# Fewer tile numbers per register load in the source stage, and ranks kept in PSUM in the target stage, of a graph network kernel

## What is computed

```python
h = jnp.maximum(_layernorm(x, axis=-1), 0.0)
x = x + _L0_gnn_ref(h, edge_index, W, att_src, att_dst, bias)   # attention over the edges of a target
h = jnp.maximum(_layernorm(x, axis=-1), 0.0)
# second layer, row = source node, col = target node
msg = jnp.concatenate([x[row], x[col], edge_attr], axis=-1)
h = jax.nn.relu(msg @ W1 + b1)
msg_out = h @ W2 + b2
out = jax.ops.segment_sum(msg_out, row, num_segments=x.shape[0])
```

## Time and profile before

| | us |
|---|---|
| median of three runs | 5765.21 |
| lowest, highest | 5764.62, 5769.41 |
| the profiled execution | 5768.6 |
| its span, first to last instruction | 5766.7 |

### The profile page before, as it was taken

How to read it: one execution, slowest core, us unless ns; L and a number is a source line. 1 busy time by engine, 2 the same in 40 slices (tenths; PEclk the granted TensorE clock), 3 DMA queues, 4 the chain that set the end, 5 groups by cost and what they waited for, 6 DMA issues and landing times.

```text
span 5766.7 us, 160506 instructions
## 1 busy us (share of the span) xinstructions
PE 5126.9 (89%) x34498; PEld 4050.5 (70%) x34499; DVE 3987.0 (69%) x14407; ACT 2886.9 (50%) x8241; POOL 3919.7 (68%) x3713
## 2 busy tenths in 40 slices
PE   4888888888888886999999999999997999999999
PEld 3677777777777774676676666666665777777777
DVE  6788878878877877555455455455445888888887
ACT  3555555555555553333333333332224777777776
POOL 4777777777777775677777777777776555555553
PEclk6888888888888887999999999999998999999999
DMA  4522222222222234998989989989896999999997
GB/s 109 161 53 53 53 53 53 52 53 52 53 52 53 53 96 140 274 274 260 268 257 259 260 261 256 264 247 268 253 256 183 211 214 212 215 214 212 214 214 188
DMA packets 859988, 990.83 MB, mean 172 GB/s; under 512 B 307992, under 2 KB 663224, under 8 KB 859774
## 3 DMA queue, kind: packets, MB, share of 16 engines
q1 hardware_dynamic: 662494, 608.23, 40.6%
q0 software_dynamic: 190592, 378.22, 24.5%
q10 hardware_dynamic: 6816, 3.38, 0.2%
HBM read 726.65 MB, written 262.76 MB: 172 GB/s over the span
## 4 chain that ended last, share of the span: by engine, by line
PE 60%; issue 10%; POOL 10%; DMA 9%; DVE 7%; DVEq 2%; ACT 2%; POOLq 0%; ACTq 0%; SPq 0%
PE bank L1700 13%; PE bank L1532 11%; PE bank L1623 9%; PE bank L1625 8%; PE bank L1690 7%; DMA xr<-arena 6%; POOL arena L495 5%; POOL xr L543 5%; PE bank L1458 2%; DMA arena<-h_tab,arena 2%; PE bank L1613 2%; PE bank L1681 1%; DVE arena L936 1%; DVE arena L1043 1%; DVEq L247 1%
## 5 line engine op out<-in xcount | busy, mean ns | idle before, releaser
L495 POOL DMA_INDIRECT arena<-h_tab,arena x1612 | 1595.4, 990 | 545.1 <-issue 406.8
L543 POOL DMA_INDIRECT xr<-arena x1612 | 1580.7, 981 | 510.6 <-issue 366.4
L1532 PE MATMUL bank<-arena 128*128 128x136 f32 x6448 | 1321.8, 334 | 76.4 <-DVE arena L1043 8.2
L704 ACT ACTIVATE arena<-bank 128x256 f32<-128x256 f32 x1612 | 591.8, 385 | 1403.1 <-PE bank L1625 923.9
L557 POOL DMA_INDIRECT arena<-p_tab,arena x428 | 668.5, 1562 | 658.7 <-DMA arena<-p_tab,arena 457.7
L1623 PE MATMUL bank<-arena 128*128 128x256 f32 x3224 | 1028.6, 401 | 92.4 <-DVE arena L1237 50.5
L1532 PEld LDWEIGHTS bank<-arena 128*128 128x128 f32 x6448 | 990.3, 216 | 159.5 <-issue 65.8
L622 ACT ACTIVATE arena<-bank 128x256 bf16<-128x256 bf16 x1612 | 618.5, 384 | 916.2 <-PE bank L1458 836.9
L1625 PE MATMUL bank<-arena 128*128 128x256 f32 x3224 | 976.4, 385 | 0.0
L1700 PE MATMUL bank<-arena 128*128 128x257 f32 x3424 | 899.0, 385 | 3.0 <-ACT arena L781 2.4
L1043 DVE TENSOR_TENSOR arena<-arena,bank 128x272 f32 x1612 | 692.1, 429 | 168.0 <-PE bank L1532 150.9
(11 more groups left out here) (254 smaller groups left out, 6438.3 us busy)
## 6 DMA issues: line engine op xcount, KB each, us to landing
arena<-xr SPq DMA_DIRECT2D x428, 516.0 KB, 3.9
arena<-q_tab SPq DMA_DIRECT2D x1612, 128.0 KB
arena<-in_edge_attr SPq DMA_DIRECT2D x61, 832.0 KB, 8.9
arena<-rel_tab SPq DMA_DIRECT2D x124, 224.0 KB
arena<-h_tab,arena POOLq DMA_INDIRECT x1612
xr<-arena POOLq DMA_INDIRECT x1612
arena<-rel_tab SPq DMA_DIRECT2D x124, 192.0 KB
xr<-arena SPq DMA_DIRECT2D x26, 516.0 KB
```

What stands on the lines that cost most here:

```text
L495: pool.indirect_dma_start(G[:, q, t, :], None, h_tab, bass.IndirectOffsetOnAxis(ap=idx[:, q, t:t + 1], axis=0)).then_inc(sem(f"gath{q}"), 16)
L543: pool.indirect_dma_start(xr, bass.IndirectOffsetOnAxis(ap=pos[:, q, t:t + 1], axis=0), Rb[:, t, :], None).then_inc(sem(f"scat{m}"), 16)
L1532: last = pe.matmul(PSB[3 + t % 2][:, k * H * MW:(k + 1) * H * MW], OH[:, (t + 2 * q) % 4, k * P:(k + 1) * P], flat(msg[:, t, :, :]), start ...
```

## The change

`pair_bins` takes the first pair and a count now. In a turn VectorE loads eight numbers from pair 8i - 4 on, which starts where it did, and TensorE eight from pair 8i - 1 on, so its loads start three numbers further on; the loads behind the loop take four numbers on VectorE and one on TensorE. In the target stage the sum of line 1203 is written into bank 5 in place; the product reads the sum there, writes `t49`, and only then TensorE gets the bank back: `rk_used` moves from the sum to the product, and a new semaphore `run_added` orders the two.

```diff
--- before.py
+++ after.py
@@ -248,10 +248,10 @@
                 bin_row[0:1, bass.ds(b * RB, count)], engines=[engine], min_val=0, max_val=NT - 1,
                 skip_runtime_bounds_check_because="a node's tile, clamped at 0")[1]
 
-        def pair_bins(engine, i):
+        def pair_bins(engine, first, count=SB):
 
             return nc.values_load_multi_w_load_instructions(
-                pbrow[0:1, bass.ds(i * SB, SB + 4)], engines=[engine], min_val=0, max_val=NT - 1,
+                pbrow[0:1, bass.ds(first + 4, count)], engines=[engine], min_val=0, max_val=NT - 1,
                 skip_runtime_bounds_check_because="counted over the bins, held under their number")[1]
 
 
@@ -1200,20 +1200,21 @@
             def rank(r, m):
                 lo, hi = m * RK, min((m + 1) * RK, BT)
                 dve.wait_ge(sem("rk_ps"), 3 * r + m + 1)
-                V.tensor_tensor(t49[:, lo:hi, :], PSB[5][:, 0:(hi - lo) * NT].rearrange("p (t b) -> p t b", b=NT),
-                                run0.unsqueeze(1).to_broadcast([P, hi - lo, NT]), ALU.add).then_inc(sem("rk_used"), 1)
+                v = PSB[5][:, 0:(hi - lo) * NT].rearrange("p (t b) -> p t b", b=NT)
+                V.tensor_tensor(v, v, run0.unsqueeze(1).to_broadcast([P, hi - lo, NT]), ALU.add).then_inc(sem("run_added"), 1)
 
             def own(r, s, m):
                 lo, hi = m * RK, min((m + 1) * RK, BT)
-                dve.wait_ge(sem("rk_used"), 3 * r + m + 1)
-                V.tensor_tensor(t49[:, lo:hi, :], t49[:, lo:hi, :], oh49[:, s, lo:hi, :], ALU.mult).then_inc(sem("own_ready"), 1)
+                dve.wait_ge(sem("run_added"), 3 * r + m + 1)
+                V.tensor_tensor(t49[:, lo:hi, :], PSB[5][:, 0:(hi - lo) * NT].rearrange("p (t b) -> p t b", b=NT),
+                                oh49[:, s, lo:hi, :], ALU.mult).then_inc(sem("rk_used"), 1)
 
             def total(r):
                 dve.wait_ge(sem("total_ps"), r + 1)
                 V.tensor_tensor(run0, run0, PSB[7][:, 64:64 + NT], ALU.add).then_inc(sem("run_ready"), 1)
 
             def reduced(r):
-                dve.wait_ge(sem("own_ready"), 3 * r + 3)
+                dve.wait_ge(sem("rk_used"), 3 * r + 3)
                 V.tensor_reduce(posf, t49, AX.X, ALU.add).then_inc(sem("posf_ready"), 1)
 
             def places(r, s):
@@ -1358,7 +1359,7 @@
                 V.tensor_tensor(a, a, PSB[4 + m % 2][:, 0:XW], ALU.add).then_inc(sem("accB_done"), 1)
 
             def sources(i, first=False, last=False):
-                regs = pair_bins(ENG.DVE, i)
+                regs = pair_bins(ENG.DVE, SB * i - 4)
                 for m in range(SB):
                     if m < SB - 1:
                         hotp(i, m + 1, first)
@@ -1374,7 +1375,7 @@
             with dve.Fori(1, NTURN - 1) as i:
                 sources(i)
             sources(NTURN - 1, last=True)
-            regs = pair_bins(ENG.DVE, NTURN)
+            regs = pair_bins(ENG.DVE, NPAIR - 4, 4)
             for m in range(SB - 4, SB):
                 if m < SB - 2:
                     add_r(NPAIR - SB + m + 2, m + 2, False)
@@ -1701,11 +1702,11 @@
                 last.then_inc(sem("seg_ps"), 1)
 
             def sources(i, first=False):
-                regs = pair_bins(ENG.PE, i)
+                regs = pair_bins(ENG.PE, SB * i - 1)
                 for m in range(SB):
                     turnp(SB * i + m, m)
                     if not (first and m < 1):
-                        source_rows(SB * i + m - 1, (m - 1) % SB, regs[m + 3], first)
+                        source_rows(SB * i + m - 1, (m - 1) % SB, regs[m], first)
                     if not (first and m < 3):
                         segment(SB * i + m - 3, (m - 3) % SB, first)
             pe.wait_ge(sem("pb_in"), 16)
@@ -1713,8 +1714,8 @@
             sources(0, True)
             with pe.Fori(1, NTURN) as i:
                 sources(i)
-            regs = pair_bins(ENG.PE, NTURN)
-            source_rows(NPAIR - 1, SB - 1, regs[3], False)
+            regs = pair_bins(ENG.PE, NPAIR - 1, 1)
+            source_rows(NPAIR - 1, SB - 1, regs[0], False)
             for m in range(SB - 3, SB):
                 segment(NPAIR - SB + m, m, False)
             pe.wait_ge(sem("accB_done"), NPAIR + 1)
```

## The result

The changed kernel takes 5866.82 us in the median of four runs (5863.24 to 5874.09), the kernel before 5767.31 beside it: a ratio of 1.0172, with 1.0156 to 1.0187 as its interval. It is **1.7% slower, by 99.5 us**, where 5726 and faster was predicted. The profiled execution of after has a span of 5866.1 us against 5766.7.

The account below looks back on a forecast made before the run. The prediction took scatter issue to bound the target stage and TensorE, delayed by register loads at turn ends, the source stage. Its terms -11.2 + 0.7 - 29 = -39.5 gave a median of 5726 us, range 5712 to 5750.

Parts of the forecast that it names:

- Eight registers for twelve: Source stage: four numbers fewer per register load save 320 ns a turn, 33.6 us over 105 loads, -29 us net.
- Rival (4): Source stage: TensorE's load from 8i + 3 costs another half load, 0.42 us a turn; 5799 us, chance 0.04.
- Product from PSUM: Target stage: with one product operand in PSUM the 46 held scatters go, -11.2 us (bounds 0 and -16.6).
- Bank 5 is released later: Next group's matmuls wait for the product, not the sum: 0 in the target stage, +0.7 us in the node stage.
- 4.5 were taken off: Source stage: part of the register loads' gain comes back as longer waits for rows, 4.5 us.
- the prediction's own sign: Source stage: VectorE's waits for rows grow beyond 92.6 us; if they double, rival (1) holds.
- rival (1): Source stage: the rows' loads take half of the gain, -14.5 instead of -29; 5740 us, chance 0.14.
- The path: Source stage: TensorE's turn gets shorter by all of the load's saving, since 320 ns is less than the 630 lost.
- the 0.63 us that the prediction says a turn loses to the load: Source stage: the sequencer sits in the register load, then issues with no lead; a pair takes 1.94 instead of 1.31 us.
- Rival (2): Register loads: price not in the numbers but, say, a fixed cost in steps; only the target stage gains, 5755, chance 0.08.
- Rival (3): Target stage: the product still holds the scatters with its one SBUF operand; -28.3, 5737 us, chance 0.06.

Follow-up runs that it names:

- the five profiles: The changed kernel with TensorE's start at 8i (twice), at 8i + 4, and at 8i with attention loads of 28, and its source-stage change alone at 8i: ratios 0.9946 to 0.9964.
- the target part alone: Kernel before with only the target stage's sum and product change, twelve registers as before: 5756.6 us, ratio 0.9990.
- the source part alone with its start mended: Kernel before with only the eight-number loads, TensorE's starting at 8i from a shifted second copy of the pair row: 5749.8 us, ratio 0.9964.
- the kernel with the start at 8i: Changed kernel, but TensorE loads its eight numbers from a shifted second copy of the pair row, starting at 8i: 5737.8 us, once more 5742.4.
- the table's kernel: Kernel before plus test register loads of various starts and counts ahead of the source stage; only load durations count, eight numbers 0.59 to 1.95 us on TensorE.

## Why the prediction was wrong

**The step that failed** is the price in *Eight registers for twelve*. It priced a load by its count alone, (2104 - 867) / 14 = 88 ns a number, and carried that price to a start that no load of TensorE or VectorE had had in the trace. Bounds were set for the price of a number, 0 to 353 ns for four, and none for the price of the start. Rival (4) named the right mechanism and the place, but sized it by a guess (half a load, 0.42 us, where the load grew by 1.07), and gave it 0.04 on the ground that loads from multiples of eight and of four take the same. That row was read correctly and was no evidence: both kinds of start are multiples of four. The runs showed in its place that TensorE's eight numbers from 8i + 3 take 1.936 us, and 0.60 to 0.64 in the five profiles with their start at 8i or 8i + 4. Rival (4) at the measured +0.98 a turn would have read 105 x 0.98 - 10 = +93, 5858.

Nor is it true, as rival (4) has it, that the trace of before holds no such start. SyncE loads seven numbers at a time from the row `rend` (line 319), which begins at a multiple of eight words, from 0, 7, 14 and so on to 42. Its row in before, and then the second and the fifth of the seven, from 7 and from 28:

```profile
L319 SPq TENSOR_LOAD <-arena x7: 1152/2739/2917, 2134.0 to 2176.2; - x7
L319 SPq TENSOR_LOAD <-arena x1: 2917/2917/2917, 2139.5 to 2139.5; - x1
L319 SPq TENSOR_LOAD <-arena x1: 2044/2044/2044, 2161.8 to 2161.8; - x1
```

The load from 0 takes 1.15 us, the one from 28 takes 2.04, and the five whose start is no multiple of four take 2.65 to 2.92. In all twelve profiles those from 0 and 28 are the shortest of the seven. SyncE's loads vary more than TensorE's, so the row would not have given the price; but that the start can cost more than a us stood in the trace, and the range could have held it.

Point by point:

- *Product from PSUM*, -11.2: measured -10.7 in after, -11.1 in the target part alone, and no held scatter in either. Right in size and mechanism; the longest scatter left takes 1.22 us. The rule of the Trainium skill that was weighed against it (SBUF — State Buffer, section Who interferes with whom: the inference that a `tensor_tensor` with two SBUF inputs does not hold the generation of descriptors) doesn't fit these runs: with two SBUF inputs 52 of 61 scatters that began during the product were longer than 0.99 us, with one, 1 of 83. Another sentence of that section, that VectorE's instructions with at most one SBUF input (outside its two-port modes) don't contend with GpSimd, agrees with the second number.
- *Bank 5 is released later*, 0 in the target stage: right; no wait of TensorE for the product shows there. +0.7 in the node stage: +0.75. An add into PSUM in place takes 0.676 us in the median, one duration and not two, as taken.
- *Eight registers for twelve* on VectorE, 0.53 expected: 0.597. With TensorE's start mended the term can be read by itself. The load falls by 0.85 - 0.59 = 0.26 us and not by 0.32, since the 88 ns came from a load with two expensive singles at its end; the price by number from whole fours is 64 ns. 105 x 0.26 = 27 us, and the source stage became shorter by 18.5, 19.7, 20.5, 24.1 and 25.0 us in the five profiles with both loads at 0.6, 21.6 in the mean. So some 5 us are given back, where 4.5 were taken off. That the two are so near is chance: the 4.5 stood for longer waits for the rows, and these don't account for it. Between 4420 and 5690 us VectorE waits 97.2 to 110.3 us for rows in the five profiles and 90.0 in before, but 79.8 in the target part alone, whose loads are those of before, and 112.1 in after, whose turns are the longest. They don't double, so by the prediction's own sign rival (1) doesn't hold; its size is not far off, 14.5 us of gain where the source part alone with its start mended gave 18.2 (14 to 28). Before, and the kernel with the start at 8i:

```profile
DVE arena L1335 <- DMA arena<-xr: 90.0, 196, 1.5
DVE arena L1340 <- DMA arena<-xr: 103.4, 210, 2.1
```

- *The path*: that TensorE's turn follows its load was right, in both directions. From 1.94 to 0.85 us of TensorE's load alone the turn falls by 1.08, and with both engines' loads from 0.87 and 0.85 to 0.60 by 0.18 to 0.23. This is why the wrong sign of the load became the wrong sign of the whole. But of the 0.63 us that the prediction says a turn loses to the load, only the part in front of the turn's end went with it (1.85 to 1.59 us in the median, where 1.58 is the value inside a turn); 0.38 us lie behind the end and stayed.
- Rival (2), a price in steps, was true of a part that decides nothing here (groups of four and singles); 12 to 8 is one group less. Rival (3) falls with the held scatters.

What remains open: of the 27 us that the two loads save some 5 don't arrive. Some 3 of them are missing already at the turns' ends, where the pair in front falls by 0.23 us in the mean of the five profiles, 24 us over 105 turns; the rest was not followed. And the loads in the loop take 0.67 to 0.70 us in the mean on TensorE's sequencer although 0.60 in the median; what lengthens some of them was not looked for.

## What to carry to other kernels

A load of several numbers into registers is cheap only if it starts at a multiple of four numbers and takes a multiple of four; loading numbers that nobody needs (28 for 26, or from 8i rather than from 8i + 3) is shorter than loading exactly those that are needed. When a change moves the start of an access, look on every engine for a row with that kind of start (here SyncE had one); if there is none, the price is unknown on the upper side too, and the range has to say so. The profile puts the idle time behind a register load down to the semaphore event that came last, or to "issue": compare the end of the load with the start of the next instruction at many turns.

## What the runs showed of the hardware

- Register loads from SBUF, on TensorE's and VectorE's sequencers alike: about 0.08 us and 64 ns a number in groups of four from a start that is a multiple of four; on TensorE 234 to 247 ns for each number from another start or left over, on VectorE 1.84 us for eight such. Twenty-six numbers take 2.11 us from 4 and 6.13 us from 2 (both in the table's kernel, the latter 6.131 to 6.137). The Trainium skill (Runtime: NRT & Kernel Launch, section Instruction fetch mechanics) gives about 200 ns a register, even for many, for loads from HBM; here, from SBUF, the singles come near that figure, and the groups of four are at a third of it.
- A product with two operands in SBUF is held itself, but not by a scatter. In the target stage of before the longest of its 183 products takes 0.707 us (median 0.662), though 159 of them start while a scatter is under way. The 1.734 us in the row below are the first product of the node stage, beside a `tensor_tensor` of GpSimd (line 522) whose operands lie in SBUF too; with one operand from PSUM the same product takes 0.67 beside the same instruction, which takes 1.74 both times. Line 1209, before and then after, and last the two engines at that place, before and then after:

```profile
L1209 DVE TENSOR_TENSOR arena<-arena x186: 449/662/1734, 2242.9 to 4328.1; 128x490 f32<-128x490 f32 x124, 128x294 f32<-128x294 f32 x62
```

```profile
L1209 DVE TENSOR_TENSOR arena<-bank,arena x186: 446/658/670, 2245.8 to 4323.0; 128x490 f32<-128x490 f32 x124, 128x294 f32<-128x294 f32 x62
```

```profile
2242.37 1.74 POOL L522 TENSOR_TENSOR arena<-arena 128x896 f32<-128x896 f32 x1 [1.03 <-DVE arena L1187]
2242.91 1.73 DVE L1209 TENSOR_TENSOR arena<-arena 128x490 f32<-128x490 f32 x1
...
2245.23 1.74 POOL L522 TENSOR_TENSOR arena<-arena 128x896 f32<-128x896 f32 x1 [1.03 <-DVE arena L1187]
2245.77 0.67 DVE L1209 TENSOR_TENSOR arena<-bank,arena 128x490 f32<-128x490 f32 x1
```

- With loads on two engines at the end of a turn, the shorter load on VectorE alone shortened the turn by 0.09 us (one profile), on both by 0.18 to 0.23. TensorE's shorter load alone was not run, so how the gain splits between the two is not shown.
